# Attention's normalisation and transpose put ahead of an expert scaling on DVE, and the out projection ahead of half a down projection on PE

## The chip, the cores and the metric

The kernel runs on one core of one Trainium2 chip. A core has five engines with programs of their own: PE (TensorE, matrix products), DVE (VectorE), ACT (ScalarE), POOL (GpSimd) and SP (SyncE, which here only issues transfers). They wait for each other by semaphores. The metric is the time on the device in microseconds (us).

## The reference

The layer is a transformer block with two branches, each modulated by a condition vector, on x of 2 x 1024 tokens with 128 features:

```python
h = _layernorm(x) * (1 + ca) + sa
x = x + ga * attention(h)     # 16 heads of 8, causal, a window of 32 keys, softmax
h = _layernorm(x) * (1 + cb) + sb
x = x + gb * ffn(h)
...
scores = xt @ gate_w                                # ffn: 8 experts, the best 2 weighted
h = gelu(einsum('td,edf->etf', xt, w1) + b1)        # 128 -> 256 in every expert
o = einsum('etf,efd->etd', h, w2) + b2              # 256 -> 128
y = _layernorm(xt + o) * ln_g + ln_b                # of every expert
out = einsum('et,etd->td', wE, y)                   # wE is zero but for two experts
```

The weights of the experts that are not chosen are zero, but all eight are computed for every token.

## The kernel before, in words

The 2048 tokens are worked off in 8 steps of 256 tokens, two tiles of 128 tokens each. Every engine has its own program, and every program is written as `front(0)` and then `body(i, ...)` for i = 0 to 8 (`steps`). The order within a body is written out by hand, engine by engine, and is what an engine follows; there is no planner. In body i three things are interleaved: the attention of step i, the second half of the FFN of step f = i - 1 (down projection, normalisation, weighting, sum over experts), and the first part of step n = i + 1 (first layernorm, q, k, v, scores). The first half of the FFN of step i (the up projections and gelus) ends the body. Body 0 has no FFN of a step before it, body 7 no next step, and body 8 only the FFN of step 7.

The down projection makes z, the input of the experts' layernorm, in four quarters q = 2 * half + tile: `down(f, q, part)` computes 4 experts for one tile of 128 tokens, in two parts, into one of two PSUM banks (q % 2). In a body, quarter 0 and 1 come among the attention's transposes, quarter 2 in two parts, and quarter 3 behind the out projection. A quarter starts with `down_start` (lines 1023 to 1025), which waits until the quarter two before it has been scaled, by the semaphore `u_done`. For each quarter ACT squares z (`square` for 0 and 1, `square_sum` for 2 and 3), DVE or ACT sums the squares, POOL turns the sums into coefficients (`coefficients`, lines 309 to 314), and DVE scales z by the coefficient and the gain into `ypart` (`scale(f, q)`, line 660, 4 instructions), which also raises `u_done`. POOL adds up the four experts of a quarter (`add_experts`, line 323, two adds) as soon as `u_done` counts it.

The attention's path around the change: PE multiplies probabilities and values (`values`, line 985; the last is `values(i, 3)`). DVE divides by the sum of the probabilities (`take_pv`, lines 608 and 609) and transposes (`turn_attn`, line 703) into `attnT`. PE multiplies by the output weights (`out_proj`, line 1048). DVE adds the result to x and takes mean and variance (`add_attn`, lines 710, 562, 565). POOL makes the inverse root of the variance (`rstd_second`, lines 339 and 340). DVE normalises (`normed_second`, line 570), PE transposes (`turn_x2`, line 1059), and DVE modulates and splits it for the FFN (`take_h2T`, lines 724 to 728). On PE, `turn_x2` stands ahead of `scores(n)`, the gate and all up projections.

POOL's program in a body runs: coefficients of quarters 0 and 1, an addition of the output bias, then

```python
if ffn and att:
    add_experts(f, 1)
    add_experts(f, 0)
if att:
    rstd_second(i)
if ffn:
    coefficients(f, 2)
```

where `add_experts(f, 1)` waits for `scale(f, 1)` by `pool.wait_ge(u_done, 4 * f + q + 1)`.

Of the kernel before, what the change touches and what calls it, by code (L numbers as in the profile page):

```python
# [29 lines left out]
def build(nc, t, out):  # L30
# [8 lines left out]
    with ctx:  # L39
# [149 lines left out]
        def bc(ap, dim, n):  # L189
            return ap.unsqueeze(dim).to_broadcast([*ap.shape[:dim], n, *ap.shape[dim:]])  # L190

        def z_bank(f, q):

            return S[q] if f == STEPS - 1 and q > 1 else zB[q % 2]
# [355 lines left out]
        def _(dve):  # L550
# [33 lines left out]
            def mask_q(n):  # L584

                dve.wait_ge(q_proj, n + 1)
                if n > 0:
                    dve.wait_ge(scored, n)
                for h in range(HG):
                    last = v.tensor_scalar(q_st[:, :, h, :], U[0][:, 0:STEP].rearrange("p (b q) -> p b q", q=BLK),  # L590
                                           b_qk[:, 0:1], headmask[:, h:h + 1], ALU.add, ALU.mult)
                last.then_inc(q_ready, 1)
# [11 lines left out]
            def take_pv(i):  # L604

                dve.wait_ge(pv_done, 4 * i + 4)
                pv = S[0][:, 0:NBLK * GROUPS * VP].rearrange("p (u v) -> p u v", v=VP)
                ca.link(v.reciprocal(rden[:, :], pv[:, :, DH]))
                ca.link(v.tensor_tensor(attn[:, :, :], pv[:, :, 0:DH], bc(rden[:, :], 2, DH), ALU.mult))

            def weights(f):

                dve.wait_ge(gexp_s, f + 1)
                cf.link(v.tensor_scalar(gden[:, :], gexp[:, :], 1.0, None, ALU.add))
                cf.link(v.reciprocal(gw[:, :, 0], gden[:, :]))
                cf.link(v.tensor_tensor(gw[:, :, 1], gexp[:, :], gw[:, :, 0], ALU.mult))
                for tt in range(TILES):
                    for j in range(2):
                        last = v.tensor_scalar(wsel[:, tt, j, :], iota[:, :], gidf[:, tt, j:j + 1],
                                               gw[:, tt, j:j + 1], ALU.is_equal, ALU.mult)  # L620
                cf.link(last)
                if f > 0:
                    dve.wait_ge(coef_s, 4 * f)
                if f > 0:
                    dve.wait_ge(wT_done, f)
                v.tensor_tensor(wexp[:, :, :], wsel[:, :, 0, :], wsel[:, :, 1, :], ALU.add).then_inc(wexp_s, 1)
# [72 lines left out]
            def turn_attn(i):  # L699

                if i > 0:
                    dve.wait_ge(o_done, i)
                v.transpose(attnT[:, :], attn[:, :, :].rearrange("p n d -> p (n d)")).then_inc(attn_ready, 1)
# [107 lines left out]
            def body(i, att, ffn, nxt):  # L811
                n, f = i + 1, i - 1
                if ffn and att:
                    weights(f)
                    zsum(f, 0)
                    weights_T(f)
                if nxt and i > 0:
                    normed_front(n)
                if ffn and att:
                    add_ln_b(f)  # L820
                    scale(f, 0)
                    zsum(f, 1)
                if nxt:
                    mask_q(n)
                if ffn and att:
                    scale(f, 1)
                if att:
                    take_pv(i)
                    turn_attn(i)
                    add_attn(i)  # L830
                    normed_second(i)
                    take_h2T(i)
                if ffn and att:
                    scale(f, 2, 0)
                if att:
                    take_gate(i)
                if ffn and att:
                    scale(f, 2, 1)
                if att:
                    top_two(i)  # L840
                if ffn and att:
                    scale(f, 3)
                if i + 2 < STEPS:
                    stats_front(n + 1)
                if nxt:
                    for s in range(GROUPS):
                        shift(n, s)
                if i == STEPS:
                    weights(f)
                    weights_T(f)  # L850
                    scale(f, 0)
                    scale(f, 1)
                    add_ln_b(f)
                    scale(f, 2)
                    add_experts(f, 1)
                    scale(f, 3)
                    add_experts(f, 3)

            steps(front, body)

        @block.tensor
        def _(pe):
# [132 lines left out]
            def down(f, q, part):  # L995

                half, tt = q // 2, q % 2
                if part == 0:
                    down_start(f, q)
                for e in range(part * HALF // 2, (part + 1) * HALF // 2):  # L1000
                    ee = half * HALF + e
                    for c in range(CH):
                        last = mm(z_bank(f, q)[:, e * D:(e + 1) * D], hid[:, ee, c, tt * P:(tt + 1) * P],  # L1003
                                  w2[:, ee * CH + c, :], start=False, stop=e == HALF - 1 and c == CH - 1,
                                  skip_group_check=True)
                if part == 1:
                    last.then_inc(z_done, 1)
# [78 lines left out]
            def body(i, att, ffn, nxt):  # L1086
                n, f = i + 1, i - 1
                if ffn and att:
                    down(f, 0, 0)
                    down(f, 0, 1)  # L1090
                if i == 0:
                    keep_warm(8)
                if att:
                    turn(i, 0)
                if ffn and att:
                    down(f, 1, 0)
                if i == 0:
                    keep_warm(2)
                if att:
                    turn(i, 1)  # L1100
                if ffn:
                    turn_weights(f)
                if i == STEPS:
                    down(f, 3, 0)
                    down(f, 3, 1)
                if i == 0:
                    keep_warm(2)
                if att:
                    values(i, 0)
                if i == STEPS - 1:  # L1110
                    keep_warm_last(2)
                if att:
                    turn(i, 2)
                if ffn and att:
                    down(f, 1, 1)
                if nxt:
                    turn_x(n)
                if ffn:
                    ln_b_sum(f)
                if att:  # L1120
                    values(i, 1)
                    turn(i, 3)
                    values(i, 2)
                if nxt:
                    proj_k(n)
                    proj_q(n)
                if ffn and att:
                    down(f, 2, 0)
                if att:
                    values(i, 3)  # L1130
                if nxt:
                    proj_v(n)
                if ffn and att:
                    down(f, 2, 1)
                if i == STEPS - 1:
                    keep_warm_last(3)
                if i == 0:
                    keep_warm(3)
                if att:
                    out_proj(i)  # L1140
                if i == 0:
                    keep_warm(8)
                if ffn and att:
                    down(f, 3, 0)
                    down(f, 3, 1)
                if att:
                    turn_x2(i)
                if nxt:
                    scores(n)
                if i == STEPS - 1:  # L1150
                    keep_warm_last(4)
                if att:
                    gate(i)
                if att:
                    up(i, 0)
                    up(i, 1)
                    up(i, 2)
                    up(i, 3)
                    up(i, 4)
                if att:  # L1160
                    up(i, 5)
                if i == STEPS - 1:
                    down(i, 0, 0)
                if att:
                    up(i, 6)
                if i == STEPS - 1:
                    down(i, 0, 1)
                if att:
                    up(i, 7)
                if i == STEPS - 1:  # L1170
                    down(i, 1, 0)
                    down(i, 1, 1)
                    down(i, 2, 0)
                    down(i, 2, 1)
# [50 lines left out]
```

## Time and profile before

| | us |
|---|---|
| median of 3 runs | 270.11 |
| the 3 runs | 268.58, 270.12, 270.11 |
| the profiled execution | 268.45 |
| its span (first to last instruction on the core) | 266.7 |
| PE busy | 235.2 (88%) |
| DVE busy | 183.2 (69%) |
| ACT busy | 159.4 (60%) |
| POOL busy | 134.7 (51%) |

The profile is of one execution. Its times are counted from the span's start. A row of a timeline gives the start, the time from there to the end of the last of the instructions merged in it, the engine, the line, the operation with output and input, and in brackets how long the engine was idle before it and which instruction ended the wait. The ends of matrix products are modelled. PEld is PE's loading of weights, which overlaps its products.

### The profile page before, as it was taken

What the parts mean: (1) busy time and instruction counts of PE and PEld (TensorE: products, weight loads), DVE (VectorE), ACT (ScalarE), POOL (GpSimd) and SP (SyncE); (2) the same over time, 40 slices, a digit from 0 to 9 for tenths busy, and PEclk for the clock granted to TensorE, in tenths of its full rate; (3) what the DMA queues carried; (4) which work ended last, traced back from release to release, by engine and by line L of the source; (5) the groups of instructions that cost most, each with busy time, mean ns of one, the idle gap of its engine ahead of it and who ended that gap; (6) DMA issues with size and microseconds to landing.
All of it is one profiled execution on the core that took longest, in us unless ns stands there. A gap on an engine that the chain in (4) does not pass through costs nothing.

```text
span 266.7 us, 7792 instructions
## 1 busy us (share of the span) xinstructions
PE 235.2 (88%) x3064; PEld 201.8 (76%) x3064; DVE 183.2 (69%) x570; ACT 159.4 (60%) x419; POOL 134.7 (51%) x254
## 2 busy tenths in 40 slices
PE   7796889998999999999999899998999999989970
PEld 3455468887888888888888788887888888858960
DVE  2989858485866677686967587677858595455175
ACT  2454408836695648744893759654884479356650
POOL 8082655247713674266714771367525660378075
PEclk9996899999999999999999999999999999999995
DMA  7930000000000000000000000000000000000000
GB/s 199 366 140 2 2 2 0 2 4 4 0 20 6 0 2 20 4 2 4 20 2 2 0 2 21 5 2 2 20 2 2 2 21 2 4 0 0 22 0 21
DMA packets 5652, 6.23 MB, mean 23 GB/s; under 512 B 336, under 2 KB 5104, under 8 KB 5360
## 3 DMA queue, kind: packets, MB, share of 16 engines
q1 hardware_dynamic: 5616, 5.74, 6.7%
q8 instruction: 24, 0.39, 0.6%
q14 instruction: 12, 0.10, 0.1%
HBM read 4.68 MB, written 1.05 MB: 21 GB/s over the span
## 4 chain that ended last, share of the span: by engine, by line
PE 47%; DVE 24%; ACT 16%; POOL 7%; issue 5%; POOLq 0%; ACTq 0%; DVEq 0%
ACT hid L484 11%; PE z L1003 6%; PE turns L867 6%; PE score L974 6%; DVE q_st L590 6%; PE score L966 5%; ACT L445 3%; DVE ypart L660 3%; PE turns L869 3%; PE turns L868 3%; DVE xn L570 3%; PE score L985 3%; PE score L1048 2%; POOL rstd L340 2%; ACT prob L445 2%
## 5 line engine op out<-in xcount | busy, mean ns | idle before, releaser
L484 ACT ACTIVATE hid<-turns,pack_ffn 128x256 f32<-128x256 f32 x128 | 50.4, 472 | 39.3 <-PE turns L869 39.3
L1003 PEld LDWEIGHTS z<-w,hid 128*128 128x128 f32 x480 | 59.4, 191 | 3.7 <-issue 1.0
L1003 PE MATMUL z<-w,hid 128*128 128x128 f32 x480 | 61.5, 276 | 0.0
L309 POOL TENSOR_SCALAR zvar<-zss 128x4 f32<-128x4 f32 x32 | 6.2, 193 | 78.4 <-DVE zss L646 69.4
L323 POOL TENSOR_TENSOR ypart<-ypart 128x256 f32<-128x256 f32 (+1 forms) x60 | 36.0, 600 | 18.4 <-DVE ypart L660 15.4
L867 PE MATMUL turns<-h_hi,w_hi 128*128 128x256 f32 x128 | 39.7, 310 | 5.0 <-ACT hid L484 4.8
L868 PE MATMUL turns<-h_lo,w_hi 128*128 128x256 f32 x128 | 35.9, 280 | 0.0
L869 PE MATMUL turns<-h_hi,w_lo 128*128 128x256 f32 x128 | 35.9, 280 | 0.0
L660 DVE SCALAR_TENSOR_TENSOR ypart<-z,zcoef,ln_gG 128x128 f32<-128x128 f32 x120 | 34.1, 341 | 1.8 <-POOL zcoef L314 1.7
L310 POOL TENSOR_TENSOR zrstd<-zvar,mhalf 128x4 f32<-128x4 f32 x32 | 33.1, 1033 | 2.7
L867 PEld LDWEIGHTS turns<-h_hi,w_hi 128*128 128x128 f32 x128 | 24.0, 188 | 9.8 <-ACT hid L484 9.5
L974 PE MATMUL score<-pack_proj,prob 128*128 128x128 f32 x128 | 21.5, 292 | 5.6 <-ACT prob L445 5.6
L451 ACT ACTIVATE probT<-score 128x512 f32<-128x512 f32 x32 | 19.1, 596 | 8.7 <-PE score L974 7.3
L868 PEld LDWEIGHTS turns<-h_lo,w_hi 128*128 128x128 f32 x128 | 24.2, 189 | 0.0
L869 PEld LDWEIGHTS turns<-h_hi,w_lo 128*128 128x128 f32 x128 | 24.1, 188 | 0.0
L445 ACT ACTIVATE prob<-sdif 128x512 f32<-128x512 f32 x32 | 19.9, 623 | 5.2 <-DVE sdif L601 5.2
L601 DVE TENSOR_TENSOR sdif<-score,smax 128x512 f32<-128x512 f32 x32 | 22.1, 692 | 1.1
L437 ACT ACTIVATE v_bd<-turns 64x512 f32<-64x512 f32 x16 | 10.1, 632 | 21.3 <-PE turns L929 21.2
L598 DVE TENSOR_REDUCE smax<-score 128x8 f32<-128x512 f32 x32 | 21.6, 676 | 1.0 <-PE score L966 1.0
L470 ACT ACTIVATE zsq<-z 128x128 f32<-128x128 f32 x64 | 16.8, 278 | 8.1 <-PE z L1003 8.0
L974 PEld LDWEIGHTS score<-pack_proj,prob 128*128 128x128 f32 x128 | 14.5, 146 | 8.6 <-ACT prob L445 8.0
L570 DVE TENSOR_SCALAR xn<-x_tokens,mv,rstd 128x128 f32<-128x128 f32 x32 | 11.4, 397 | 11.0 <-POOL rstd L340 9.6
(143 smaller groups left out, 454.7 us busy)
## 6 DMA issues: line engine op xcount, KB each, us to landing
w<-in_w SPq DMA_DIRECT2D x2, 1024.0 KB, 7.2
out_x<-yout SPq DMA_DIRECT2D x8, 128.0 KB, 1.8
x_tokens<-in_x SPq DMA_DIRECT2D x1, 896.0 KB, 6.7
ln_g<-in_ln_g SPq DMA_DIRECT2D x1, 512.0 KB
pack_mod<-in_pack_mod SPq DMA_DIRECT2D x1, 385.0 KB, 3.0
pack_proj<-in_pack_proj SPq DMA_DIRECT2D x1, 193.0 KB, 4.3
pack_att<-in_pack_att SPq DMA_DIRECT2D x1, 130.5 KB, 4.2
x_tokens<-in_x SPq DMA_DIRECT2D x1, 128.0 KB, 2.9
```

What stands on the lines that cost most here:

```text
L310: cf.link(g.tensor_tensor(zrstd[:, b, :], zvar[:, b, :], mhalf[:, 0:HALF], ALU.pow))
L323: cf.link(g.tensor_tensor(ypart[:, tt, at:at + n, :], ypart[:, tt, at:at + n, :], ypart[:, tt, at + n:at + 2 * n, :], ALU.add))
L445: a.activation(prob[:, s, :], sdif[:, s, :], ACT.Exp, scale=float(DH) ** -0.5).then_inc(exped, 1)
L484: last = a.activation(hid[:, e, c, :], U[(e + 1) % 2][:, c * STEP:(c + 1) * STEP], ACT.Gelu, bias=b1[:, e, c:c + 1])
L598: ca.link(v.reduce_max(smax[:, s % 2, :], sc, axis=AX))
L601: v.tensor_tensor(by_key(sdif[:, s, :]), sc, bc(smax[:, s % 2, :], 2, KEYS), ALU.subtract).then_inc(shifted, 1)
L660: last = v.scalar_tensor_tensor(ypart[:, tt, ee, :], z_bank(f, q)[:, e * D:(e + 1) * D], zcoef[:, q % 2, e:e + 1], ln_gG[:, b, ee, :], ALU ...
L867: mm(outp, a_hi, b_hi, start=True, stop=False)
L868: mm(outp, a_hi, b_lo, start=False, stop=False)
L869: return mm(outp, a_lo, b_hi, start=False, stop=True)
L974: last = tr(S[s][:, m * P:(m + 1) * P], prob[:, s, m * P:(m + 1) * P], ident[:, :])
L1003: last = mm(z_bank(f, q)[:, e * D:(e + 1) * D], hid[:, ee, c, tt * P:(tt + 1) * P], w2[:, ee * CH + c, :], start=False, stop=e == HALF - 1 ...
```

## The change

Two steps are moved in the body's order, one on DVE and one on PE. POOL's, ACT's and SP's programs, and all instructions and waits themselves, stay the same.

```diff
--- before.py
+++ after.py
@@ -822,11 +822,12 @@
                     zsum(f, 1)
                 if nxt:
                     mask_q(n)
-                if ffn and att:
-                    scale(f, 1)
                 if att:
                     take_pv(i)
                     turn_attn(i)
+                if ffn and att:
+                    scale(f, 1)
+                if att:
                     add_attn(i)
                     normed_second(i)
                     take_h2T(i)
@@ -1130,8 +1131,6 @@
                     values(i, 3)
                 if nxt:
                     proj_v(n)
-                if ffn and att:
-                    down(f, 2, 1)
                 if i == STEPS - 1:
                     keep_warm_last(3)
                 if i == 0:
@@ -1141,6 +1140,7 @@
                 if i == 0:
                     keep_warm(8)
                 if ffn and att:
+                    down(f, 2, 1)
                     down(f, 3, 0)
                     down(f, 3, 1)
                 if att:
```

DVE, in body 3: the scaling of quarter 1 (L660), `take_pv` (L608, L609), the transpose (L703) and `add_attn` (L710 on). Before:

```order
L590 TENSOR_SCALAR q_st<-turns,pack_proj,pack_att 128x8x32 x4
L660 SCALAR_TENSOR_TENSOR ypart<-z,zcoef,ln_gG 128x128 x4
L608 RECIPROCAL rden<-score 128x32
L609 TENSOR_TENSOR attn<-score,rden 128x256
L703 STREAM_TRANSPOSE attnT<-attn 128x256
L710 TENSOR_TENSOR x_tokens<-x_tokens,score 128x256
L562 BN_STATS stats<-x_tokens 128x6 x2
```

and with the change:

```order
L590 TENSOR_SCALAR q_st<-turns,pack_proj,pack_att 128x8x32 x4
L608 RECIPROCAL rden<-score 128x32
L609 TENSOR_TENSOR attn<-score,rden 128x256
L703 STREAM_TRANSPOSE attnT<-attn 128x256
L660 SCALAR_TENSOR_TENSOR ypart<-z,zcoef,ln_gG 128x128 x4
L710 TENSOR_TENSOR x_tokens<-x_tokens,score 128x256
L562 BN_STATS stats<-x_tokens 128x6 x2
```

The four instructions of the scaling have moved behind the transpose; they stand between it and the addition that waits for PE's out projection.

PE, in body 3, from the last product with the values (L985; with the change L986, as the lines there are shifted by one) to the second transposes. Before:

```order
L985 MATMUL score<-v_bd,probT 32x2x9 x16
L929 MATMUL turns<-pack_att,hT 64x128 x8
L1003 MATMUL z<-w,hid 128x128 x4
L1048 MATMUL score<-w_oG,attnT 128x128 x2
L1023 MATMUL z<-center_r,h_hi 128x512
L1024 MATMUL z<-center_r,h_lo 128x512
L1025 MATMUL z<-b_rows,ones_r 128x512
L1003 MATMUL z<-w,hid 128x128 x8
L1059 MATMUL turns<-pack_proj,xn 128x128 x2
```

and with the change:

```order
L986 MATMUL score<-v_bd,probT 32x2x9 x16
L930 MATMUL turns<-pack_att,hT 64x128 x8
L1049 MATMUL score<-w_oG,attnT 128x128 x2
L1004 MATMUL z<-w,hid 128x128 x4
L1024 MATMUL z<-center_r,h_hi 128x512
L1025 MATMUL z<-center_r,h_lo 128x512
L1026 MATMUL z<-b_rows,ones_r 128x512
L1004 MATMUL z<-w,hid 128x128 x8
L1060 MATMUL turns<-pack_proj,xn 128x128 x2
```

The out projection's products (L1048, now L1049) stand directly behind the value projection of the next step, and the four experts' second half (L1003, now L1004) behind them, followed at once by quarter 3.

## Rows read from the trace of the kernel before

**Rows 1.** The page: the chain that ended last, by engine, whole program.
```profile
PE 47%; DVE 24%; ACT 16%; POOL 7%; issue 5%; POOLq 0%; ACTq 0%; DVEq 0%
```

**Rows 2.** Busy time by window: steps 1 and 6; then PEclk, DMA share, GB/s.
```profile
46.80:75.90 29.10, 27.27 (x377) 24.27 (x376) 20.74 (x68) 19.31 (x51) 14.84 (x29) 1.00 0.02 7
...
192.00:221.00 29.00, 27.18 (x375) 24.17 (x375) 21.00 (x65) 19.21 (x51) 13.93 (x27) 1.00 0.02 6
```

**Rows 3.** Timeline of DVE, step 3: start us, duration us, what [idle before, releaser].
```profile
114.69 1.90 DVE L590 TENSOR_SCALAR q_st<-turns,pack_proj,pack_att 128x256 f32<-128x256 f32 x4 [0.35 <-PE turns L919]
116.51 1.12 DVE L660 SCALAR_TENSOR_TENSOR ypart<-z,zcoef,ln_gG 128x128 f32<-128x128 f32 x4
117.54 0.35 DVE L608 RECIPROCAL rden<-score 128x32 f32<-128x32 f32 x1
...
118.39 0.45 DVE L703 STREAM_TRANSPOSE attnT<-attn 128x256 f32<-128x256 f32 x1
119.64 0.42 DVE L710 TENSOR_TENSOR x_tokens<-x_tokens,score 128x256 f32<-128x256 f32 x1 [0.81 <-PE score L1048]
...
120.61 0.25 DVE L565 BATCH_NORM_AGGREGATE mv<-stats 128x2 f32<-128x6 f32 x2
122.07 0.60 DVE L570 TENSOR_SCALAR xn<-x_tokens,mv,rstd 128x128 f32<-128x128 f32 x2 [1.21 <-POOL rstd L340]
...
124.48 0.60 DVE L660 SCALAR_TENSOR_TENSOR ypart<-z,zcoef,ln_gG 128x128 f32<-128x128 f32 x2
```

**Rows 4.** Timeline of PE, step 3.
```profile
116.17 0.45 PE L985 MATMUL score<-v_bd,probT 128*32 128x18 f32 x32
...
117.57 1.16 PE L1003 MATMUL z<-w,hid 128*128 128x128 f32 x8
118.89 0.71 PE L1048 MATMUL score<-w_oG,attnT 128*128 128x128 f32 x4 [0.16 <-DVE attnT L703]
119.35 0.48 PE L1023 MATMUL z<-center_r,h_hi 128*128 128x512 f32 x1
...
120.14 1.95 PE L1003 MATMUL z<-w,hid 128*128 128x128 f32 x16
122.73 0.44 PE L1059 MATMUL turns<-pack_proj,xn 128*128 128x128 f32 x2 [0.65 <-DVE xn L570]
```

**Rows 5.** Timeline of POOL, step 3, and in the last row the kernel's end.
```profile
117.71 2.61 POOL L323 TENSOR_TENSOR ypart<-ypart 128x256 f32<-128x256 f32 x4 [1.03 <-DVE ypart L660]
121.02 0.22 POOL L339 TENSOR_SCALAR var<-mv 128x2 f32<-128x2 f32 x1 [0.70 <-DVE mv L565]
121.32 0.71 POOL L340 TENSOR_TENSOR rstd<-var,mhalf 128x2 f32<-128x2 f32 x1
122.12 0.19 POOL L309 TENSOR_SCALAR zvar<-zss 128x4 f32<-128x4 f32 x1
...
123.48 0.20 POOL L314 TENSOR_TENSOR zcoef<-zrstd,wexp 128x4 f32<-128x4 f32 x1
...
260.46 2.85 POOL L323 TENSOR_TENSOR ypart<-ypart 128x256 f32<-128x256 f32 x4
```

**Rows 6.** Chain of waits, step 3: start us, us, what.
```profile
121.32 0.72 POOL rstd L340
```

**Rows 7.** Timeline of ACT, step 3.
```profile
119.91 0.22 ACT L470 ACTIVATION_READ_ACCUMULATOR zsq<-z 128x1 f32 x1
...
126.63 1.57 ACT L484 ACTIVATE hid<-turns,pack_ffn 128x256 f32<-128x256 f32 x4 [3.37 <-PE turns L869]
```

**Rows 8.** Timeline of PE and POOL, step 7.
```profile
232.12 0.45 PE L985 MATMUL score<-v_bd,probT 128*32 128x18 f32 x32
...
237.00 0.22 POOL L339 TENSOR_SCALAR var<-mv 128x2 f32<-128x2 f32 x1 [0.71 <-DVE mv L565]
```

**Rows 9.** Page: granted clock in 40 slices (tenths); timeline of PE, start.
```profile
PEclk9996899999999999999999999999999999999995
...
22.44 1.12 PE L974 MATMUL score<-pack_proj,prob 128*128 128x128 f32 x4 [2.22 <-ACT prob L445]
...
35.54 0.44 PE L1059 MATMUL turns<-pack_proj,xn 128*128 128x128 f32 x2 [1.33 <-DVE xn L570]
```

More of the change, by code:

```diff
@@ L824, in body @@
                     mask_q(n)
+                if att:
+                    take_pv(i)
+                    turn_attn(i)
                 if ffn and att:
@@ L827, in body @@
                 if att:
-                    take_pv(i)
-                    turn_attn(i)
                     add_attn(i)
```

## The prediction

> **What bounds the kernel now.** I read the page's chain by engine and line first. The chain that ended last is spread over PE, DVE, ACT and POOL, and issue time is only 5% [rows 1]. So no engine is full: the time is a relay, and what counts is who hands over to whom in each pass. Next I cut the span into passes of 29.0 to 29.1 us: those of step 1 and step 6 (and the four between) hold PE busy 27.27 and 27.18, DVE 20.74 and 21.00, ACT 19.31 and 19.21, all at a granted clock of 1.00 [rows 2], so one pass can be read for all. I took step 3 (f = 2), from 114 to 125 us, and read it engine by engine.
>
> DVE [rows 3]: mask_q ends at 114.69 + 1.90 = 116.59. Then scale(f, 1) stands at 116.51, take_pv at 117.54, the transpose at 118.39 (ended 118.84), after it a gap of 0.81 for PE, add_attn at 119.64, the statistics' last instruction at 120.61 (ended 120.86), a gap of 1.21 for POOL, and the second normalisation at 122.07.
>
> PE [rows 4]: the values product begins at 116.17 and ends at 116.62, the second half of the third quarter runs from 117.57, the out projection starts at 118.89 after a wait of 0.16, down(f, 3) runs from 119.35 to 120.14 + 1.95 = 122.09, and then PE sits for 0.65 until the normalised tokens come, at 122.73.
>
> POOL [rows 5]: four adds of expert outputs (experts of quarter 1, then of quarter 0) start at 117.71, 0.08 after scale(f, 1) ended at 116.51 + 1.12 = 117.63, and last 2.61, to 120.32. POOL then waits 0.70 for DVE's statistics, and var and rstd run at 121.02 and 121.32. This rstd is on the chain of waits [rows 6], and what it releases, turn_x2, stands on PE in front of the scores of the next step, the gate and the FFN. Whatever delays rstd here therefore delays the whole pass, while 0.70 us of lateness of the four adds costs nothing. That slack of 0.70 is the number the change hangs on.
>
> **The change, part by part.** No instruction is added or removed, and POOL's, ACT's and SP's programs stay as they are. Step 0 has no FFN part and step 8 no attention part, so it touches the seven passes of steps 1 to 7.
>
> (a) *take_pv and the transpose ahead of scale(f, 1).* The values' product ends at 116.62 [rows 4]; DVE followed PE's last out projection by 0.04 (118.89 + 0.71 = 119.60 to 119.64), so take_pv can start at 116.66, just behind mask_q. From take_pv's start to the transpose's end is 118.84 - 117.54 = 1.30 [rows 3]. attnT is ready at 117.96 in place of 118.84: 0.88 earlier.
>
> (b) *scale(f, 1) behind them.* It needs z coefficients that came before it could start at 116.51, so no new wait. A DVE instruction starts up to 0.08 before its forerunner's recorded end (116.59 to 116.51), so it stands at 117.88 and ends 1.12 later, at 119.00, in place of 117.63: 1.37 later. Two engines wait for it. PE's down(f, 3) waits for z's second bank; it would be reached at 119.36 (next item), so 0.36 of cover are left. POOL's four adds wait for it too, and behind them in POOL's program stand rstd, and the coefficients of quarters 2 and 3.
>
> (c) *PE's out projection ahead of down(f, 2, 1).* PE ends the value projection for the next step (proj_v) and starts the third quarter's second half at 117.57. That half no longer fills the time up to attnT, so PE idles there for about 0.4, which is hidden as PE has slack later. The out projection starts at 117.96 + 0.05 = 118.01; 0.46 later (118.89 to 119.35) the eight matmuls of the half start, about half of the sixteen's 1.95 without the last one's drain, some 0.89; down(f, 3) starts at 119.36 against 119.35, thus where it was, and ends at 122.1. The squares of quarter 2 on ACT wait for that half. They ended at 119.91 + 0.22 = 120.13 and would now end near 120.8, with the table load and the last squares moved by some 0.2 to 0.7; ACT sat idle for 3.37 before the first gelu, at 126.63 [rows 7], which covers it.
>
> (d) *add_attn.* The out projection is done at 118.01 + 0.71 = 118.72, DVE is free only at about 118.96 after scale. add_attn starts there, 0.68 earlier than 119.64, and the statistics end at 120.18.
>
> (e) *POOL.* The four adds start 0.08 after scale's end, at 119.08, and end 2.61 later, at 121.69. The statistics are ready at 120.18, 1.5 us before that. POOL's next instruction starts 0.09 after its forerunner (121.32 + 0.71 = 122.03 to 122.12 [rows 5]), so var starts at 121.78 in place of 121.02. **0.76 us later per pass.** The gain of 0.68 in (d) is gone, since rstd stands behind the adds. DVE's normalisation and PE's turn_x2 move with it: PE would sit from 122.1 to 123.49, 1.4 us in place of 0.65. Everything behind turns up 0.76 later: the two coefficients on POOL also by 0.76, still ahead of DVE, which took scale(f, 2) 0.80 after they were there (123.48 + 0.20 to 124.48 [rows 3, 5]).
>
> That POOL holds to its program can be seen here. Between 120.32 and 121.02 POOL was idle although the squares of quarter 2 had been ready since 120.13 [rows 7]; their zvar ran only at 122.12, behind rstd [rows 5]. The Trainium skill says the same against this change, in TensorE: Matmul & The Clock Gate, section Architectural detail: GpSimd's queue is a strict FIFO. By that rule rstd waits for the adds (+0.76 a pass); an engine that took what is ready would give -0.68. By that rule, the trace agrees.
>
> (f) *Step 7.* mask_q is not there, but the product of the values ends at 232.12 + 0.45 = 232.57 and var stood at 237.00 [rows 8]. From the product's end to var the new order needs what it needs in step 3, 121.78 - 116.62 = 5.16, so 237.73: 0.73 later. Step 8 only inherits the shift.
>
> Sum: 6 x 0.76 + 0.73 = **5.3 us later**. Bounds of one pass: if take_pv issues straight behind mask_q (116.51) it is 0.61, together 4.3; if the four adds take 2.85 as they do at the kernel's end [rows 5], beside DVE work, it is 1.0, together 7.0.
>
> The profiled execution took 268.45 us (span 266.70). The three timed ones were 268.58, 270.11 and 270.12. They scatter over two levels 1.5 apart, so I add to the mean of all four, 269.3: 269.3 + 5.3 = **274.6 us**. Against the median of 270.11 that would be 275.4, against the profiled one 273.8.
>
> **Rivals.**
>
> 1. *rstd is not held by the adds* (faster). The relay then gains (d): attention's result 0.68 earlier, PE free at 122.05 just in time; 7 x 0.68 = 4.8, giving 264.5 us. It decides where POOL's adds end before the statistics at 120.18, which would need them to be over 1.1 us after scale ends; they take 2.61, in this pass and in step 7 alike. Against it also stands the idle POOL of 120.32 to 121.02. Chance 0.04.
>
> 2. *The delay is taken up again* (within 1%). If some engine after turn_x2 had its own late input, a part of the 0.76 would vanish there. For it: ACT must finish its table load and squares before the first gelu. Against it: 3.37 us of idleness there, and PE had nothing between turn_x2 and the scores. With 0.3 a pass left it is +2.1, 271.4 us. Chance 0.08.
>
> 3. *Nothing moves*, since the values' product comes so late that take_pv has to wait and scale could as well run. It comes 0.03 after mask_q, so no: chance 0.03, 269.3 us.
>
> 4. *PE's clock falls* (much slower). The granted clock of 40 slices is 9 to full but for 20.0 to 33.3 us, where it is 0.6 and 0.8, between the levels of 1.2 and 2.4 GHz [rows 9]; PE had waited 2.22 us ahead of 22.44. It had waited 1.33 us ahead of 35.54 too, and there the slice holds 9. The new gap of 1.4 is like the second. If it fell all the same, the PE work from 122.73 to the first gelu at 126.63, 3.9 us on the chain, would take up to twice as long: 5.3 + 7 x 3.9 = 33, so 302 us. The Trainium skill (TensorE: Matmul & The Clock Gate, the section on the HAM clock gate) has idleness lower the clock; what that would make here is this rival's 302 us, against 274.6 at a clock that holds. Chance 0.02.
>
> **How the numbers follow.** The forecast has 0.83, the rivals 0.04, 0.08, 0.03 and 0.02. The forecast's own spread is 268.45 + 4.3 = 272.7 to 270.11 + 7.0 = 277.1; I take 272.5 to 277.1, which leaves the rivals out (0.17). A change under 1%, 2.7 us, can't be told from none here. Rival 1 is the faster case, 0.04; rivals 2 and 3 are the same, with a little of the forecast's lower edge, 0.12; the rest, 0.84, is slower.
>
> **What would show it.** In the changed profile: attnT's transpose ends some 1.3 us after the values' product; the out projection waits up to 0.4 for it; POOL's first add of quarter 1 comes some 2.4 us after that product; var follows the last add at 0.09 without a wait for DVE's statistics, DVE's wait for rstd grows from 1.21 to about 2.65 (122.83 less 120.18), and PE waits 1.4 in place of 0.65 ahead of turn_x2; passes of 29.8 us. I am wrong if var still starts after an idle POOL, if the adds take well under 2.6, if down(f, 3) starts with a wait for scale, or if a later stretch of the pass has become shorter.

## The result, and the profile after

The changed kernel is slower, and by more than forecast: the ratio to the kernel before is 1.038 (95% interval 1.031 to 1.045).

| | before | changed |
|---|---|---|
| median, us | 270.04 | 280.35 |
| lowest and highest, us | 268.58, 270.12 | 277.82, 281.44 |
| profiled execution, us (span) | 268.45 (266.7) | 280.17 (278.4) |
| DVE's statistics to var on POOL, step 3, us | 0.16 | 1.65 |
| PE's wait ahead of turn_x2, step 3, us | 0.65 | 1.35 |

I first looked at whether the forecast's steps are there. Timeline of DVE in step 3 of the changed kernel, against [rows 3]:

```profile
117.54 1.90 DVE L590 TENSOR_SCALAR q_st<-turns,pack_proj,pack_att 128x256 f32<-128x256 f32 x4 [0.35 <-PE turns L920]
119.54 0.36 DVE L608 RECIPROCAL rden<-score 128x32 f32<-128x32 f32 x1
...
120.39 0.45 DVE L703 STREAM_TRANSPOSE attnT<-attn 128x256 f32<-128x256 f32 x1
120.76 1.08 DVE L660 SCALAR_TENSOR_TENSOR ypart<-z,zcoef,ln_gG 128x128 f32<-128x128 f32 x4
121.76 0.41 DVE L710 TENSOR_TENSOR x_tokens<-x_tokens,score 128x256 f32<-128x256 f32 x1
...
122.72 0.25 DVE L565 BATCH_NORM_AGGREGATE mv<-stats 128x2 f32<-128x6 f32 x2
125.67 0.60 DVE L570 TENSOR_SCALAR xn<-x_tokens,mv,rstd 128x128 f32<-128x128 f32 x2 [2.70 <-POOL rstd L340]
...
130.46 0.17 DVE L682 COPY gsc<-turns 128x16 f32<-128x16 f32 x1 [1.78 <-PE turns L1070]
```

take_pv follows mask_q, the transpose ends at 120.84, scale(f, 1) stands behind it, and add_attn is no longer released by PE but starts as scale ends. The statistics end at 122.97, and then DVE waits 2.70 us for rstd, where it waited 1.21. Timeline of POOL, same step, against [rows 5]:

```profile
121.92 2.61 POOL L323 TENSOR_TENSOR ypart<-ypart 128x256 f32<-128x256 f32 x4 [2.40 <-DVE ypart L660]
124.62 0.22 POOL L339 TENSOR_SCALAR var<-mv 128x2 f32<-128x2 f32 x1
124.92 0.71 POOL L340 TENSOR_TENSOR rstd<-var,mhalf 128x2 f32<-128x2 f32 x1
```

The four adds waited for scale(f, 1), last the same 2.61 us, and var follows them with no idle time, though its input was ready 1.65 us earlier. Timeline of PE, against [rows 4]:

```profile
119.02 0.45 PE L986 MATMUL score<-v_bd,probT 128*32 128x18 f32 x32
119.39 1.09 PE L930 MATMUL turns<-pack_att,hT 128*64 128x128 f32 x16
120.89 0.71 PE L1049 MATMUL score<-w_oG,attnT 128*128 128x128 f32 x4 [0.41 <-DVE attnT L703]
121.44 1.06 PE L1004 MATMUL z<-w,hid 128*128 128x128 f32 x8
122.25 0.48 PE L1024 MATMUL z<-center_r,h_hi 128*128 128x512 f32 x1
...
123.03 1.95 PE L1004 MATMUL z<-w,hid 128*128 128x128 f32 x16
126.33 0.44 PE L1060 MATMUL turns<-pack_proj,xn 128*128 128x128 f32 x2 [1.35 <-DVE xn L570]
...
126.93 2.54 PE L967 MATMUL score<-kT,q_st 32*128 32x64 f32 x64
129.40 1.02 PE L1070 MATMUL turns<-pack_ffn,h2T 128*128 128x8 f32 x4
130.27 0.56 PE L868 MATMUL turns<-h_hi,w_hi 128*128 128x256 f32 x1
```

The out projection waits 0.41, turn_x2 1.35. Up to here every row is as forecast. The last three are not: the 64 products of the scores take 2.54 us (1.91 in step 3 of the kernel before), the gate's four (L1070) 1.02 (0.61 before), and the first FFN products have grown too. The page's line of the granted clock, against [rows 9], and then the time from one var (L339) to the next, the last stretch split at turn_x2 (columns: stretch, length, busy time of PE, PEld, DVE, ACT, POOL with counts, granted clock, DMA share, GB/s):

```profile
PEclk9999899999999999996899999999999869999997
```

```profile
94.80:124.62 29.82, 27.05 (x377) 24.17 (x376) 21.07 (x68) 19.16 (x51) 14.82 (x30) 1.00 0.02 6
124.62:157.02 32.40, 30.25 (x381) 27.23 (x380) 21.10 (x68) 19.59 (x51) 14.66 (x29) 0.89 0.02 6
186.84:216.66 29.82, 27.05 (x377) 24.17 (x376) 21.05 (x68) 19.16 (x51) 14.82 (x29) 1.00 0.02 6
216.66:248.71 32.05, 29.21 (x360) 25.79 (x359) 18.03 (x58) 17.41 (x47) 13.09 (x27) 0.89 0.02 6
```

```profile
126.33:134.90 8.57, 8.57 (x100) 8.28 (x101) 6.11 (x26) 2.06 (x6) 5.55 (x12) 0.60 0.01 3
```

From var to var it was 29.07 us in the kernel before (91.96 to 121.02 to 150.10). Now an undisturbed pass takes 29.82, 0.75 more, against 0.76 forecast. Two of the seven passes take 32.40 and 32.05, at a mean granted clock of 0.89: in each PE's clock is lowered for a while, soon after the wait ahead of turn_x2. The clock has two levels, 2.4 GHz (1.00) and 1.2 GHz (0.50). Both times it falls 1.6 to 1.8 us after turn_x2 starts and stays at the lower level for 6.8 us, PE being busy throughout (the mean of 0.60 over 8.57 us, above, is made of both levels); these two stretches lie inside the lowered ones:

```profile
128.05:134.55 6.50, 6.50 (x53) 6.38 (x49) 4.59 (x24) 1.71 (x5) 3.80 (x8) 0.50 0.00 0
220.40:226.90 6.50, 6.50 (x46) 6.38 (x43) 4.75 (x20) 2.14 (x6) 3.85 (x9) 0.50 0.00 1
```

The FFN's products stand 0.21 us apart there in place of 0.12. Such a pass costs 32.40 - 29.82 = 2.58 us more.

So the 11.7 us between the two profiled executions come apart as 7 x 0.75 = 5.3 for the queue on POOL, 2 x 2.58 = 5.2 for the clock, and some 1.3 from the start of the program: the first transpose, ahead of anything the change moves, starts at 32.10 in place of 31.27, and step 0's clock was 0.94 in place of 1.00. These 1.3 us belong to the single execution and not to the change: the first var stands at 33.83 in the kernel before and at 35.17 in the changed one, but at 33.78 in a variant below (two products ahead of the out projection) whose step 0 is that of the changed kernel.

### The profile page after: what moved, and what is told of

Same layout as the page of the kernel before. It is cut to its first block, busy times and chain, and to the rows that moved or that the text cites. A ratio compares the mean times of both kernels' runs of the same rounds, so it can differ in the third digit from the quotient of the medians.

```text
span 278.4 us, 7792 instructions
## 1 busy us (share of the span) xinstructions
PE 242.0 (87%) x3064; PEld 208.9 (75%) x3064; DVE 182.2 (65%) x570; ACT 159.4 (57%) x419; POOL 134.5 (48%) x254
## 4 chain that ended last, share of the span: by engine, by line
PE 53%; DVE 15%; ACT 14%; POOL 10%; issue 5%; DMA 1%; POOLq 0%; ACTq 0%; DVEq 0%
ACT hid L484 8%; PE z L1004 8%; POOL ypart L323 7%; PE turns L868 7%; PE score L975 5%; PE score L967 5%; PE turns L870 4%; PE turns L869 4%; PE score L986 4%; ACT L445 3%; DVE ypart L660 3%; DVE xn L570 2%; POOL rstd L340 2%; PE turns L1070 2%; ACT prob L445 2%
## 5 line engine op out<-in xcount | busy, mean ns | idle before, releaser
L484 ACT ACTIVATE hid<-turns,pack_ffn 128x256 f32<-128x256 f32 x128 | 51.2, 471 | 51.1 <-PE turns L870 50.5
L1004 PEld LDWEIGHTS z<-w,hid 128*128 128x128 f32 x480 | 59.4, 191 | 2.6
L1004 PE MATMUL z<-w,hid 128*128 128x128 f32 x480 | 60.8, 275 | 0.0
L868 PE MATMUL turns<-h_hi,w_hi 128*128 128x256 f32 x128 | 41.9, 327 | 3.9 <-ACT hid L484 3.5
L869 PE MATMUL turns<-h_lo,w_hi 128*128 128x256 f32 x128 | 37.8, 295 | 0.0
L870 PE MATMUL turns<-h_hi,w_lo 128*128 128x256 f32 x128 | 37.7, 294 | 0.0
L660 DVE SCALAR_TENSOR_TENSOR ypart<-z,zcoef,ln_gG 128x128 f32<-128x128 f32 x120 | 33.9, 338 | 0.1
L868 PEld LDWEIGHTS turns<-h_hi,w_hi 128*128 128x128 f32 x128 | 26.0, 204 | 8.7 <-ACT hid L484 8.2
L869 PEld LDWEIGHTS turns<-h_lo,w_hi 128*128 128x128 f32 x128 | 26.2, 205 | 0.0
L870 PEld LDWEIGHTS turns<-h_hi,w_lo 128*128 128x128 f32 x128 | 26.1, 204 | 0.0
L975 PE MATMUL score<-pack_proj,prob 128*128 128x128 f32 x128 | 20.6, 283 | 4.8 <-ACT prob L445 4.7
L570 DVE TENSOR_SCALAR xn<-x_tokens,mv,rstd 128x128 f32<-128x128 f32 x32 | 10.6, 372 | 21.3 <-POOL rstd L340 20.0
```

The source lines that it names most:

```text
L484: last = a.activation(hid[:, e, c, :], U[(e + 1) % 2][:, c * STEP:(c + 1) * STEP], ACT.Gelu, bias=b1[:, e, c:c + 1])
L660: last = v.scalar_tensor_tensor(ypart[:, tt, ee, :], z_bank(f, q)[:, e * D:(e + 1) * D], zcoef[:, q % 2, e:e + 1], ln_gG[:, b, ee, :], ALU ...
L868: mm(outp, a_hi, b_hi, start=True, stop=False)
L869: mm(outp, a_hi, b_lo, start=False, stop=False)
L870: return mm(outp, a_lo, b_hi, start=False, stop=True)
L975: last = tr(S[s][:, m * P:(m + 1) * P], prob[:, s, m * P:(m + 1) * P], ident[:, :])
```

## The experiments

The experiments test one account, called theory Q: rstd is queued behind the adds (0.76 a pass), and the rest of the loss is the clock. Every ratio is to the kernel before, run on the same chip.

**1. Each half of the change alone.** DVE's half is the first hunk of the change's diff, PE's half the other two.

```diff
 e1: only DVE's                      e2: only PE's
     take_pv(i)                      -    down(f, 2, 1)        # behind proj_v
     turn_attn(i)                         out_proj(i)
+    scale(f, 1)                     +    down(f, 2, 1)
     add_attn(i)                          down(f, 3, 0)
```

Expected of DVE's half:

> Only DVE's half of the change: take_pv and the transpose ahead of scale(f, 1); PE's order as before. Theory Q (rstd queued behind POOL's four adds, 0.76 us a pass, 5.3 in all, and the rest of the loss is a granted clock that falls in some passes after PE's new gap): POOL's adds start as late as in the changed kernel, so var is 0.76 later again and undisturbed passes take 29.8 us; PE has no gap ahead of the out projection but one of 1.7 ahead of turn_x2 (in place of 0.41 and 1.35), so the clock falls in some passes too: 275 to 283 us. Rival P (the loss comes from PE's half, the half quarter that no longer covers attnT): time of the kernel before, 269 to 270, passes of 29.1.

Measured: 280.45 us, 1.039 (1.034 to 1.044). The whole loss is in DVE's half. The two slow passes and an undisturbed one between them (from var to var):

```profile
65.52:98.06 32.54, 30.28 (x375) 27.38 (x374) 21.20 (x68) 19.59 (x50) 14.65 (x30) 0.90 0.02 6
98.06:127.88 29.82, 27.19 (x375) 24.24 (x374) 21.15 (x68) 19.27 (x50) 14.82 (x30) 1.00 0.02 6
157.72:190.29 32.57, 30.40 (x375) 27.39 (x374) 21.16 (x68) 19.70 (x50) 14.81 (x29) 0.90 0.02 6
```

PE's wait ahead of turn_x2 is 1.62 here, and the clock falls again, in passes 1 and 4 (a pass has the number of the step whose var it starts with). In pass 1:

```profile
67.23 0.44 PE L1060 MATMUL turns<-pack_proj,xn 128*128 128x128 f32 x2 [1.62 <-DVE xn L570]
```

Expected of PE's half:

> Only PE's half of the change: the out projection ahead of down(f, 2, 1); DVE's order as before. Theory Q: attnT comes at its old time, PE waits 1.3 us for it in place of 0.35, the half quarter and quarter 3 end 0.9 later, at about 123.0 of step 3, turn_x2 starts 0.1 to 0.3 later: 1 to 2 us in all, 270.5 to 272 us, and more only if the clock falls after the gap of 1.3. POOL's var starts as before. Rival P: nearly the whole loss, 277 us and more.

Measured: 269.96 us, 1.001 (0.998 to 1.003), no difference. The theory gave 1 to 2 us of loss; by the interval there is at most 0.9. Timeline of PE and one pass:

```profile
116.84 1.09 PE L929 MATMUL turns<-pack_att,hT 128*64 128x128 f32 x16
119.18 0.71 PE L1048 MATMUL score<-w_oG,attnT 128*128 128x128 f32 x4 [1.24 <-DVE attnT L703]
...
121.32 1.95 PE L1003 MATMUL z<-w,hid 128*128 128x128 f32 x16
123.10 0.38 PE L1059 MATMUL turns<-pack_proj,xn 128*128 128x128 f32 x2
```

```profile
121.31:150.41 29.10, 26.82 (x379) 24.15 (x378) 21.06 (x68) 19.17 (x52) 14.96 (x29) 1.00 0.02 6
```

PE now waits 1.24 ahead of the out projection, quarter 3 comes later, and turn_x2 follows it with no wait: the half quarter only changed the side of the out projection on which PE idles. Passes of 29.10 are 0.03 longer than before. In none of them does the clock fall. Nor does it behind a longer gap in step 7, 1.57 us, where no work of a next step follows; from there to 246 us it stays at 1.00:

```profile
235.25 0.71 PE L1048 MATMUL score<-w_oG,attnT 128*128 128x128 f32 x4 [1.57 <-DVE attnT L703]
```

Rival P is out.

**2. POOL's order.** In the changed kernel rstd and the coefficients go ahead of the adds, which nobody waits for soon:

```diff
-                if ffn and att:
-                    add_experts(f, 1)
-                    add_experts(f, 0)
                 if att:
                     rstd_second(i)
                 ...
                 if ffn:
                     coefficients(f, 3)
                 if ffn and att:
+                    add_experts(f, 1)
+                    add_experts(f, 0)
                     add_experts(f, 2)
```

> The changed kernel, with POOL's order in a body changed: rstd_second, coefficients of quarters 2 and 3, and only then the four adds of quarters 1 and 0. Theory Q: rstd starts 0.16 behind the statistics, 0.68 earlier than in the kernel before, PE's gap ahead of turn_x2 is about 0 and the clock holds: passes of 28.4 us, 269.3 - 4.8 = 264.5 us. Rival P (the loss sits in the new order of PE and DVE, and POOL's adds have part in it only by chance): 275 us or more.

Measured: 264.33 us, 0.980 (0.974 to 0.985). Its timelines of POOL, DVE and PE in step 3:

```profile
119.93 0.22 POOL L339 TENSOR_SCALAR var<-mv 128x2 f32<-128x2 f32 x1 [3.54 <-DVE mv L564]
...
121.03 0.19 POOL L309 TENSOR_SCALAR zvar<-zss 128x4 f32<-128x4 f32 x1
```

```profile
117.63 1.09 DVE L659 SCALAR_TENSOR_TENSOR ypart<-z,zcoef,ln_gG 128x128 f32<-128x128 f32 x4
...
119.59 0.25 DVE L564 BATCH_NORM_AGGREGATE mv<-stats 128x2 f32<-128x6 f32 x2
120.98 0.60 DVE L569 TENSOR_SCALAR xn<-x_tokens,mv,rstd 128x128 f32<-128x128 f32 x2 [1.14 <-POOL rstd L340]
```

```profile
117.76 0.71 PE L1048 MATMUL score<-w_oG,attnT 128*128 128x128 f32 x4 [0.40 <-DVE attnT L702]
...
119.90 1.95 PE L1003 MATMUL z<-w,hid 128*128 128x128 f32 x16
121.68 0.40 PE L1059 MATMUL turns<-pack_proj,xn 128*128 128x128 f32 x2
...
122.24 1.91 PE L966 MATMUL score<-kT,q_st 32*128 32x64 f32 x64
```

var starts 0.09 behind the statistics, PE does not wait ahead of turn_x2, and passes are 28.27 us with the clock at 1.00. The edit brings the coefficients of quarters 2 and 3 forward as well as rstd, but DVE did not wait for those in the changed kernel either: there they are ready at 127.28 and 128.92, and the scalings that use them start at 128.08, without a wait, and at 130.55, behind a wait for PE. The same kernel in more rounds:

> The changed kernel with POOL's new order once more, in more rounds, to narrow its ratio: 264.3 us, 0.980 of the kernel before, at most 0.005 to either side.

264.10 us, 0.981 (0.979 to 0.984). This version beats both kernels, by 5.6 us and by 16.

The control, POOL's new order in the kernel before:

> The kernel before with POOL's new order alone (rstd_second and the coefficients of quarters 2 and 3, then the adds of quarters 1 and 0). Theory Q: in the kernel before POOL is idle for 0.70 us ahead of var, so its order costs nothing there; passes of 29.07, the time of the kernel before within 0.5 us. Rival S (the order of POOL is worth 5 us by itself, and the changed order of DVE and PE adds nothing): 264 to 266 us.

269.26 us, 0.998 (0.996 to 1.001): no difference, since POOL was idle ahead of var there. Rival S is out. So the gain needs both, DVE's order and POOL's. And with those two, but PE's order as in the kernel before:

> DVE's half of the change with POOL's new order, and PE's order as before. Theory Q: the out projection starts 0.46 later than in the changed kernel, behind the half quarter; DVE's addition starts some 0.24 later; passes of 28.5 us, 266 us. If PE's half is worth nothing once POOL is out of the way: 264.3 us as with it.

266.44 us, 0.987 (0.980 to 0.994), passes of 28.57 to 28.59: PE's half is worth 0.3 us a pass once POOL is out of the way, and nothing before.

**3. A dose.** Only the adds of quarter 0 are moved behind:

```diff
                 if ffn and att:
                     add_experts(f, 1)
-                    add_experts(f, 0)
                 ...
                 if ffn and att:
+                    add_experts(f, 0)
                     add_experts(f, 2)
```

> The changed kernel, with only the adds of quarter 0 taken behind rstd and the coefficients; those of quarter 1 stay ahead of rstd. Theory Q, as a dose: POOL's work between scale(f, 1) and var is 1.30 in place of 2.61, so var starts near 120.47 of step 3, 0.55 earlier than in the kernel before and about 0.1 later than with both pairs behind: passes of 28.4 us, 265 us, clock at 1.00. If what counts is only that POOL waits for scale at all ahead of rstd: 274 us or more.

265.09 us, 0.985 (0.979 to 0.991). Timeline of POOL:

```profile
118.05 1.27 POOL L323 TENSOR_TENSOR ypart<-ypart 128x256 f32<-128x256 f32 x2 [2.40 <-DVE ypart L660]
119.40 0.22 POOL L339 TENSOR_SCALAR var<-mv 128x2 f32<-128x2 f32 x1
```

With 1.27 us of adds in front, passes are 28.49 (28.4 expected); with 2.61 in front they are 29.82; with none, 28.27. The steps are unequal, as a queue makes them: half the adds end only 0.22 behind DVE's statistics (119.32 against 119.10), all four end 1.56 behind them (124.53 against 122.97), and only what lies behind the statistics costs time.

**4. The clock.** PE's gap ahead of turn_x2 is filled with products of zeros, in steps 1 to 6:

```diff
                     down(f, 3, 1)
+                if ffn and nxt:
+                    pe.wait_ge(q_ready, n + 1)
+                    for _ in range(5):
+                        mm(U[0][:, :], idle[:, 0:P], idle[:, :], start=True, stop=True)
                 if att:
                     turn_x2(i)
```

> The changed kernel, with five products of zeros (bf16, 128 x 512) on PE ahead of turn_x2 in steps 1 to 6, in PE's gap of 1.35 us. Their result is not read. Theory Q: they end before the normalised tokens come, so they cost nothing; the granted clock stays at 1.00 in all middle passes, each 29.8 us, and the time is 274.6 us (what the prediction gave without a fall of the clock). Rival R (the slow stretches have a cause that PE's gap has no part in): 280 us as the changed kernel, with the same slow passes.

274.05 us, 1.016 (1.012 to 1.021), all five runs from 273.8 to 275.3. Timeline of PE in the gap (the first of the five products has no record), and the pass that was slow in the changed kernel:

```profile
125.27 1.03 PE L1149 MATMUL turns<-idle 128*128 128x512 bf16 x4
126.58 0.44 PE L1060 MATMUL turns<-pack_proj,xn 128*128 128x128 f32 x2 [0.28 <-DVE xn L570]
```

```profile
124.87:154.71 29.84, 28.06 (x385) 24.59 (x385) 21.07 (x68) 19.17 (x51) 14.87 (x29) 1.00 0.02 6
```

Added work on PE makes the kernel 6 us faster than the changed one, with passes of 29.8 as before and no fall. That is the 274.6 of the forecast, and Rival R is out.

Then only the small gap is filled, two products ahead of the out projection:

```diff
+                if ffn and nxt:
+                    pe.wait_ge(q_ready, n + 1)
+                    for _ in range(2):
+                        mm(U[0][:, :], idle[:, 0:P], idle[:, :], start=True, stop=True)
                 if att:
                     out_proj(i)
```

> The changed kernel, with two products of zeros on PE ahead of the out projection in steps 1 to 6, in PE's gap of 0.41 us, and nothing in the gap of 1.35 ahead of turn_x2. Theory T (the clock falls after the gap of 1.35, whatever comes ahead of the out projection): one to three slow passes remain, 277 to 282 us. Rival U (the two gaps count only together, as 1.76): the clock holds in all middle passes, 274.3 us.

279.24 us, 1.038 (1.032 to 1.044), with two slow passes (from transpose to transpose; one undisturbed pass between):

```profile
89.19:121.57 32.38, 30.33 (x378) 27.30 (x376) 21.06 (x69) 19.45 (x50) 14.83 (x29) 0.89 0.02 6
121.57:151.40 29.83, 27.47 (x382) 24.30 (x380) 21.05 (x69) 19.16 (x50) 14.83 (x29) 1.00 0.02 6
181.22:213.60 32.38, 30.23 (x378) 27.21 (x376) 21.05 (x69) 19.38 (x50) 14.82 (x29) 0.89 0.02 6
```

The gap ahead of turn_x2, 1.34 to 1.36 there, is enough by itself; Rival U is out. One more run puts one product into it in place of five:

> As the run with five products of zeros in PE's gap ahead of turn_x2, but with one product in it: it starts where quarter 3 ends and leaves a gap of about 1.15 us in place of 1.35. If the length of this gap decides (the run with PE's half alone had a gap of 1.24 and no slow pass), the clock holds: passes of 29.8, 274 us. If a gap of this length is already too long, one to three slow passes stay: 277 to 281 us.

275.16 us, 1.025 (1.019 to 1.030). The profiled run, 275.13, had no fall in its passes, nor, by their times, had two others (274.98 and 275.19); the fourth took 277.82 at a mean clock of 0.964 in place of 0.985, so it most likely had one. The inserted product itself has no record in this trace, so the gap shows as 1.36; the load of its weights has one in each of these gaps:

```profile
124.74 0.10 PEld L1149 LDWEIGHTS turns<-idle 128*128 128x128 bf16 x1
```

The gap of about 1.15 us is therefore an estimate. Both outcomes that were named came true in part: the clock held in three runs and most likely fell once in the fourth. Together with the gap of 1.57 in PE's half alone, behind which it held, this says that the length of the gap alone does not set whether the clock falls.

## Why the prediction was wrong

The direction and the mechanism of the forecast's sum were right; the time, 280.35 us, was not in the range of 272.5 to 277.1, because a second cost came on top. Point by point:

- (a) to (d), DVE and PE: right. The transpose ends 1.37 after the values' product (1.3), the out projection waits 0.41 (0.4), down(f, 3) starts without a wait for scale, add_attn starts as scale ends.
- (e), rstd behind the adds: right, 0.75 a pass in place of 0.76, and shown by taking the adds away (28.27), halving them (28.49) and leaving them (29.82). The 264.5 us that rival 1 priced for a rstd that is not held is what POOL's other order gives, 264.1. What the Trainium skill says of GpSimd's queue (TensorE: Matmul & The Clock Gate, section Architectural detail), a strict FIFO, agrees with a var that starts at 124.62 with its input there at 122.97.
- (f), step 7: it would have been 0.7 as forecast. From var to var the last pass of the changed kernel holds the second fall, but in the run with the filled gap step 7 is 29.48 against 28.76 before.
- The sum, 5.3: right as far as it goes. The kernel with a filled gap, where the clock held, takes 274.05.
- **The step that failed is rival 4, the clock, which was put at 0.02 and left out of the range.** It read two rows, a wait of 2.22 with a fall and a wait of 1.33 without one [rows 9], concluded "The new gap of 1.4 is like the second", and gave a fall 0.02. One wait of 1.33, in a step without FFN work, was no evidence for seven of 1.35 in other surroundings. All four timed runs of the changed kernel show a mean clock of 0.946 to 0.964; those of the kernel before show 0.975 to 0.988, but for one of 0.964 that took 271.09 us. What (e) itself worked out, PE idle for twice as long seven times over, was the very condition of this rival. (Its reading of the clock line also left out the last slice of the kernel before, 0.5; nothing in the argument hangs on it.)
- Its price was off as well, on the other side: it was all or nothing, 33 us for falls in all seven passes. The profile shows two falls of 2.6 each, 5.2. The 3.9 that it set for a fall took the clock as low from turn_x2 to the first gelu. But the first 1.6 us of that stretch still ran at 1.00: from turn_x2's start to the first gelu it is 3.88 us in an undisturbed pass (96.51 to 100.39) and 5.61 in the slow one (126.33 to 131.94, below), 1.73 more. The other 0.85 of the 2.58 come behind the first gelu. There PE otherwise waits some 0.2 us for a gelu after every 12 up projections, in which a part of its slowness disappears.

```profile
131.94 0.84 ACT L484 ACTIVATE hid<-turns,pack_ffn 128x256 f32<-128x256 f32 x2 [5.72 <-PE turns L870]
```

What stays open is why two passes of seven fall and the others not, with a gap of 1.35 in each of steps 1 to 7. In the three traces with two falls they lie three passes apart (passes 3 and 6, 1 and 4, 2 and 5); what else differs between the passes no row shows.

The Trainium skill's section on the HAM clock gate (TensorE: Matmul & The Clock Gate) has idleness lower the clock, and the fill of the gap that removed the falls agrees with it. How short a gap can be followed by a fall is told here by the runs, 1.35 us, and not by that page.

## What to carry to other kernels

When an instruction is moved later, follow its semaphore to the engine that waits for it, and read what is queued behind that wait: here a scaling that moved by 1.4 us held four adds that nobody needed, and these held an inverse root that everybody needed. Such a chain can turn a loss into a gain by one more swap: DVE's reorder cost 4% alone, gained 1.3% together with POOL's, and 1.9% with PE's half as well.

A new wait on PE has a second price, the clock behind it. If a sum makes PE's gaps longer than any that the same stretch of the trace holds without a fall, the fall belongs into the range at a real chance, priced per pass and not for all of them.

## What was not expected of the hardware

- PE work that computes nothing made the kernel faster: five bf16 products of zeros a pass, in a gap of 1.35 us, took the time from 280.4 to 274.1 us.
- Gaps of PE of 1.22 to 1.25 us (PE's half alone, ahead of the out projection, steps 1 to 6) and one of 1.57 (its step 7) left the clock at 1.00. Of seven gaps of 1.35, and of seven of 1.62, two each were followed by a fall.
- In all six falls behind such gaps that the traces hold, the clock stayed at 0.50 for 6.8 us although PE was busy. It costs less than half of that: the pass took 2.58 us longer.
